# Batch 0's first pass: the keys' adds from the fourth key on move to GpSimd, rotations go two tokens ahead

## The reference

```
def step(Sc, inp):
    a11, a12, bt, k, v = inp
    S0, S1 = (Sc[..., 0], Sc[..., 1])
    r0 = a11[..., None] * S0 + a12[..., None] * S1
    r1 = -a12[..., None] * S0 + a11[..., None] * S1
    Sr = jnp.stack([r0, r1], -1)
    err = v - jnp.sum(k * Sr, -1)
    Sn = Sr + bt[..., None, None] * err[..., None] * k
    return (Sn, Sn)
```

## Time and profile before

| | |
|---|---|
| median of 3 runs | 1620.52 us (1620.04 to 1621.19) |
| profiled execution, own time | 1622.55 us |
| its span | 1620.3 us |
| VectorE busy | 1250.8 us, 77% |
| TensorE matmul busy | 1283.6 us, 79% |
| ScalarE busy | 432.4 us, 27% |
| GpSimd busy | 67.1 us, 4% |
| batch 0's first pass, first state product to the scan's begin | 175.3 to about 343 us |

### The profile page before, as it was taken

The page is one execution under the profiler, slowest core; times in us unless marked ns, Lnnn a source line. Parts: engine busy times, 40 slices in busy tenths (PEclk is TensorE's granted clock), DMA queues, the critical chain, the costliest instruction groups (busy, mean ns, idle before and its releaser), DMA issues. The chain is left out here.

```text
span 1620.3 us, 12609 instructions
## 1 busy us (share of the span) xinstructions
PE 1283.6 (79%) x4244; PEld 748.8 (46%) x4244; DVE 1250.8 (77%) x1996; ACT 432.4 (27%) x660; POOL 67.1 (4%) x32
## 2 busy tenths in 40 slices
PE   3970777734887978598599999887888885899997
PEld 1540333321444446245366666553444453566665
DVE  4899999989999966869989999899999857010111
ACT  2442110100002043444533232330020143332332
POOL 0000121200000000000001111000000000000000
PEclk9995899976999989799799999998999987999999
DMA  4000101030111021300022222323111100322221
GB/s 156 1 7 0 52 39 52 26 130 0 39 39 52 13 109 52 111 1 7 26 92 91 91 91 78 104 91 117 52 39 39 52 1 1 98 78 78 78 73 71
DMA packets 51679, 94.37 MB, mean 58 GB/s; under 512 B 4641, under 2 KB 39841, under 8 KB 50721
## 3 DMA queue, kind: packets, MB, share of 16 engines
q1 hardware_dynamic: 51616, 93.58, 16.6%
HBM read 73.64 MB, written 19.92 MB: 58 GB/s over the span
## 5 line engine op out<-in xcount | busy, mean ns | idle before, releaser
L502 PE MATMUL ps<-wshare,uT 128*128 128x512 f32 x512 | 245.0, 634 | 55.8 <-DVE kz L1383 55.7
L609 PE MATMUL ps<-kz 128*128 128x256 f32 x1024 | 243.8, 381 | 14.2 <-ACT kz L809 12.5
L595 PE MATMUL ps<-kz 128*128 128x512 f32 x512 | 245.3, 603 | 7.4 <-DVE coef L990 4.1
L609 PEld LDWEIGHTS ps<-kz 128*128 128x128 f32 x1024 | 195.1, 191 | 96.6 <-issue 60.6
L502 PEld LDWEIGHTS ps<-wshare,uT 128*128 128x128 f32 x512 | 101.4, 203 | 179.7 <-issue 118.0
L809 ACT ACTIVATE kz<-ps,small 128x512 f32<-128x512 f32 x128 | 87.6, 686 | 306.3 <-PE ps L595 306.1
L433 PE MATMUL ps<-wshare,xnT 128*128 128x512 f32 x256 | 119.2, 609 | 56.2 <-ACT ps L673 56.2
L1541 DVE TENSOR_TENSOR kz<-ps,b_s 128x256 f32<-128x256 f32 x16 | 6.3, 414 | 180.7 <-PE ps L609 180.7
L595 PEld LDWEIGHTS ps<-kz 128*128 128x128 f32 x512 | 99.1, 194 | 85.9 <-issue 75.8
L744 ACT ACTIVATE kz<-ps 128x512 f32<-128x512 f32 x32 | 19.1, 597 | 371.4 <-PE ps L487 371.4
L865 POOL TENSOR_TENSOR work<-work 128x1024 f32<-128x1024 f32 x28 | 66.9, 2390 | 954.4 <-DVE work L1277 656.4
(11 more groups left out here) (261 smaller groups left out, 1881.4 us busy)
## 6 DMA issues: line engine op xcount, KB each, us to landing
kz<-in_w SPq DMA_DIRECT2D x128, 256.0 KB, 2.9
kap_d<-kz SPq DMA_DIRECT2D x26, 512.0 KB, 2.7
kz<-kap_d SPq DMA_DIRECT2D x26, 512.0 KB, 3.2
uT<-in_x SPq DMA_DIRECT2D x8, 512.0 KB, 5.5
wshare<-in_wq SPq DMA_DIRECT2D x2, 2048.0 KB, 7.7
kz<-in_x SPq DMA_DIRECT2D x2, 2048.0 KB, 13.2
coef<-in_x SPq DMA_DIRECT2D x2, 2048.0 KB, 7.7
wshare<-in_wk SPq DMA_DIRECT2D x2, 1024.0 KB, 11.0
```

Source lines behind the costliest of these rows:

```text
L502: t = mm(ps[:, 2 * (j % 2) + c, :], uT3[:, k, j * P:(j + 1) * P], wq_s[:, k, c, :], start=(k == 0), stop=(k == KI - 1))
L595: t = mm(ps[:, 4 + i % 2, :], w1_r[r][:, k, (f % 2) * P:(f % 2 + 1) * P], x2T[:, k, n * 512:(n + 1) * 512], start=(k == 0), stop=(k == KM ...
L609: t = mm(ps[:, 6 + q // 2, (q % 2) * DM:(q % 2 + 1) * DM], hbuf(i)[:, q * P:(q + 1) * P], w2_r[r][:, f % 2, :], start=(f == 0 and q % 2 == ...
```

## The change

In batch 0, on VectorE: the rotation of key 2 and its add are done in step 1, right behind X; at the end of step i (to i = 13) the halves of key i+2 are made instead of those of key i+1, and VectorE no longer adds them. On GpSimd: behind the sum of step i (to i = 13) a second instruction adds the halves of key i+2 into its ring buffer and releases `k_ready`; it waits for the second half (`kq_used`) and for the store of the key that had the buffer (`k_stored`). On TensorE: key(i+1) stands ahead of update(i-1); in step 1 the order is key(1), update(0), key(2).

```diff
@@ keys (TensorE)
-                        key(b, i)
-                        if b == 0:
-                            update(i - 1)
+                        if b > 0:
+                            key(b, i)
+                        else:
+                            if i == 1:
+                                key(b, 1)
+                                update(0)
+                            if i + 1 < L:
+                                key(b, i + 1)
+                            if i >= 2:
+                                update(i - 1)
@@ GpSimd
+            R = wshare[:, 0:2048].rearrange("p (a i n) -> p a i n", a=2, i=2)
...
                     nc.gpsimd.tensor_tensor(PSt[:, :, 2], PSt[:, :, 2], Z, ALU.add).then_inc(sum_ready, 1)
+                    if b == 0 and i + 2 < L:
+                        pool.wait_ge(kq_used, i + 3)
+                        if i + 2 >= KR1:
+                            pool.wait_ge(k_stored[(i + 2) % KR1], k_stored_count(b, i + 2 - KR1))
+                        nc.gpsimd.tensor_tensor(k1(i + 2), R[:, :, 0], R[:, :, 1], ALU.add).then_inc(k_ready, 1)
@@ pass_1 (VectorE)
                     tt(X, M, kb, MUL).then_inc(x_ready, 1)
+                    if b == 0 and i == 1:
+                        rotate(2, 0)
+                        rotate(2, 1)
+                        rotated(2)
...
                     product(i, g)
                     if b == 0 and more:
-                        rotate(i + 1, 0)
-                        rotate(i + 1, 1)
-                        rotated(i + 1)
+                        if i + 2 < L:
+                            rotate(i + 2, 0)
+                            rotate(i + 2, 1)
```

## The result

The changed kernel was timed three times, each beside the kernel before on the same chip (the ratio is changed over before):

| | changed, median (range) | before, median | ratio, 95% interval |
|---|---|---|---|
| first | 1607.10 (1604.26 to 1607.86) | 1620.71 | 0.9912 [0.9897, 0.9928] |
| second | 1605.09 (1604.70 to 1605.82) | 1621.31 | 0.9900 [0.9885, 0.9915] |
| third | 1605.59 (1604.40 to 1606.88) | 1622.27 | 0.9895 [0.9879, 0.9912] |

What follows compares the result with a forecast made beforehand. VectorE was taken to bound batch 0's first pass. Of 19.6 us removed about 5 are given back at start and end, leaving 14.4: 1620.52 - 14.4 = 1606.1 us, own range 1603.6 to 1608.2, with most of two rivals 1603 to 1611.5.

Steps and rivals of the forecast that it cites:

- What is removed: VectorE's key add in batch 0's first pass: 1.51 us a key, step 11.24 to 9.73, at most 19.6 us.
- TensorE in the steady state: TensorE keeps up with 9.73 us steps: state ready at +9.14, 0.59 before X; the 1.94 us gap shrinks to 0.43.
- Rival B: TensorE's clock goes on falling in 6 of 12 steps, costing 6.7 us in all: 1612.8 us; chance 0.08.
- GpSimd and the cover: GpSimd's key add follows its sum and takes 2.62 us under X and value, which cover 2.81; nothing is lost.
- the 0.1 that I allowed: Assumed price, 0.1 us, of two GpSimd instructions behind each other, between the sum and the key's add.
- The margin of 0.19: Room between GpSimd's key add, needing 2.62 us, and the 2.81 us that X and value on VectorE cover.
- Rival A: GpSimd's second add starts late and holds g by 0.3 to 0.8 us a step: 1610 to 1616 us; chance 0.14.
- The rule that I quoted: VectorE instructions with two SBUF inputs and GpSimd instructions reading SBUF exclude each other; at most one SBUF input is free.
- The start: First steps of the pass: 1.25 us stall at key 2, and X(2) at 190.65 instead of 186.54.
- The end: Last step: update(14) at low clock takes 5.40 us, VectorE stalls 3.4, X(15) comes 10.84 after X(14).
- the worse end: Both clock prices at their worst, update(14) as slow as 6.66 us: X(15) at 320.29, time 1608.2 us.
- The sum: X(15) at 318.25 against 332.64, 14.4 us earlier, carried one for one to the end: 1606.1 us.

Runs made afterwards that it cites:

- experiment 6: The changed kernel's new order alone, rotations two tokens ahead but all keys added on VectorE: 1624.36 us, ratio 1.0013 to the kernel before.
- the fillers at the end: The changed kernel with six useless matmuls of 512 columns between the last key and the last update on TensorE: 1605.24 us, ratio 0.9900 to the kernel before.
- experiments 4 and 5: Changed kernel with batch 0's value product behind g: 1607.61 us; with a useless GpSimd add of 256 or 1280 columns before each key add: 1610.47 or 1636.83 us.

## Why the prediction was right, step by step

- **What is removed.** 1.51 a key and a step of 9.73: measured 9.72 to 9.74 in 36 steps of three profiles. The split was not as I had it: by experiment 6, 0.20 of the 1.51 belongs to the order, probably the semaphore turn ahead of X, and 1.31 to the add.
- **TensorE in the steady state.** The state was to be ready at +9.14. With the fillers at the end, where VectorE waits for it at the full clock, X to X is 9.06, so it is ready 0.66 before it is needed. The gap of 1.94, behind which 6 of 14 updates had taken 5.40, shrank to 0.43 as worked out, and no update between the second and the last took 5.40. Rival B fell with it.
- **GpSimd and the cover.** The add follows the sum without the 0.1 that I allowed and ends 0.24 before g. The margin of 0.19 in the prediction leaves that 0.1 out; with it, it would have been 0.11. And the rows of before show only the two rotations beside a sum, at 1.22 each, not X: that X passes beside a GpSimd add was first shown by the changed kernel. Rival A did not happen, and its mechanism is real: its price is the overlap less 0.13 or 0.14 (experiments 4 and 5). The rule that I quoted from the Trainium skill, "SBUF — State Buffer", "Who interferes with whom", holds here in both orders, GpSimd first (g 2.67) and VectorE first (GpSimd's add 3.32), but for those 0.13 or 0.14 us, and its counterpart too: an X with one operand in PSUM beside a GpSimd add stays at 2.28.
- **The start.** 1.25 at key 2: measured 1.2. X(2) at 190.65, the middle of 189.85 and 191.43: measured 191.09, 191.23 and, without the clock's fall, 189.98. The middle did not occur in these profiles; the two ends did, to 0.34 us, and the granted clock at key 3 (0.53 and 0.58 in the late ones, 1.00 in the early one) tells them apart.
- **The end.** X(15) 10.84 after X(14): measured 11.96, 11.82 and 12.02. This term was mis-sized, by 1.0 to 1.2 us: the last update takes 6.60, 6.46 and 6.66. I took 5.40 from updates behind a 1.94 us wait, where the wait here is 5.6 us and the nearer row was the first key behind its long wait, 6.66, which the prediction had as the worse end.
- **The sum.** X(15) at 318.25: measured 319.75, so 12.9 us of the 14.4. The medians came out within 1.0 us of 1606.1, and that closeness is in part luck: the pass gave 0.2 to 1.6 us less than forecast, and up to 2.6 behind it and 0.45 outside the span, which no step of the prediction had, made up for it. With the same way behind the pass as before, the pass alone gives 12.8 to 14.2 us, 1606.3 to 1607.7, still within the stated range.

## What to carry to other kernels

A move to an idle engine is worth what the loaded engine gives up, less the waits that the moved work had covered: here 19.6 us taken out of VectorE's steps brought 13 in the pass, and of the 6.7 given back some 4 were TensorE behind an idle stretch at the half clock (1.2 at key 3, 2.9 at the last update). Place GpSimd's work beside VectorE instructions that read one operand from PSUM, and count the cover in tenths of a microsecond; here there is room for the two adds, and a third of 256 columns already cost 0.32 us a step. Rotate far enough ahead that the slower engine's result is wanted a step later, and look at the first and the last step of such a pipeline by themselves.

## What the runs showed that I had not expected

Two GpSimd adds behind each other start 2.31 or 2.32 us apart at 2.35 us each (from the second pair on), so a pair has no gap. A VectorE add held by a GpSimd add is longer by 0.11 at an overlap of 0.24, by 0.31 at 0.45 and by 1.45 at 1.59 (244.16 - 242.57), so the last 0.13 to 0.14 us of GpSimd's row, as the profile draws it, hold nobody. VectorE's own rows overlap by some 0.1 us too, so that may be how ends are recorded and not when the hold ends. And useless matmuls ahead of the last update brought X(15) 2.8 to 3.0 us nearer to X(14) in all three profiles that have them.
